# A transformer layer on eight cores: more buffers, one small DMA on another queue, one matmul moved, transposes two deep

## The reference, cut to what matters

```python
q, k, v = (proj(wq), proj(wk), proj(wv))          # 16 heads of 128
q, k = apply_rope(q, k, sin, cos)
att = softmax(einsum('bhqd,bhkd->bhqk', q, k) / sqrt(128))
y = einsum('bhqk,bhkd->bhqd', att, v)
x = _layernorm(x + y @ wo.T)
gate = silu(_qlinear(x, wq_gate, s_gate))         # W = (wq - 128) * scale
up = _qlinear(x, wq_up, s_up)                     # 5632 hidden features
x = _layernorm(x + _qlinear(gate * up, wq_down, s_down))
```

## Time and profile before

| | us |
|---|---|
| device time, the two runs shown | 5102.63 and 5252.95 (median 5177.79) |
| profiled execution, its own time | 5106.49 |
| its span on the slowest core (core 6) | 5104.6; all cores 5094.1 to 5104.6 |
| TensorE busy | 3883.1 (76%) |
| ScalarE, VectorE busy | 1315.2 (26%), 635.9 (12%) |
| mean granted TensorE clock | 0.869 of full |
| V projection and its end | 510 to 912 |
| attention | 912 to 2437 |
| output projection (1024 matmuls, 223.8 us) | 2437 to 2675 |
| first and second half of the feed-forward | 2760 to 3896, 3965 to 5105 |
| TensorE idle before the halves | 99.3 and 220.2 |

### The profile page before, as it was taken

The page is one execution under the profiler, slowest core; times in us unless marked ns, Lnnn a source line. Parts: engine busy times, 40 slices in busy tenths (PEclk is TensorE's granted clock), DMA queues, the critical chain, the costliest instruction groups (busy, mean ns, idle before and its releaser), DMA issues.

```text
span 5104.6 us, 42263 instructions; the slowest of 8 cores (5094.1 to 5104.6 us)
## 1 busy us (share of the span) xinstructions
PE 3883.1 (76%) x15680; PEld 1486.5 (29%) x15680; DVE 635.9 (12%) x1592; ACT 1315.2 (26%) x1073; POOL 393.9 (8%) x744
## 2 busy tenths in 40 slices
PE   4999656677777777777983999998830999998870
PEld 2444222111111111111431444433310444443320
DVE  1222000000000000000220000112121000101122
ACT  0111010333333333333341333310022333320003
POOL 0000000000000000000000000012200000002210
PEclk9999878777777777777996999999965999999985
DMA  6334111100100100100455444434425344434432
GB/s 110 59 81 101 44 41 36 34 13 13 25 13 13 25 13 13 25 13 5 140 179 98 76 80 76 75 63 60 62 71 125 64 79 78 75 67 62 62 50 115
DMA packets 193545, 310.96 MB, mean 61 GB/s; under 512 B 92097, under 2 KB 145474, under 8 KB 184514
## 3 DMA queue, kind: packets, MB, share of 16 engines
q0 software_dynamic: 99392, 188.99, 23.3%
q1 hardware_dynamic: 93954, 119.28, 7.5%
HBM read 412.86 MB, written 58.72 MB: 92 GB/s over the span
## 4 chain that ended last, share of the span: by engine, by line
PE 63%; DMA 20%; issue 6%; ACT 5%; DVE 5%; another core or an unknown queue 1%; DVEq 0%; POOLq 0%; ACTq 0%; SPq 0%; POOL 0%
PE PS L555 12%; PE PS L562 12%; PE PS L453 9%; DMA AB<-wd_c 9%; PE PS L509 6%; PE PS L505 5%; PE PS L468 5%; PE PS L537 4%; PE PS L490 4%; DMA AB<-AB 3%; ACT AB L609 3%; DMA v_sp<-AB 3%; PE PS L493 3%; DMA AB<-x1b 2%; PE PS L576 2%
## 5 line engine op out<-in xcount | busy, mean ns | idle before, releaser
L555 PE MATMUL PS<-AB 128*128 128x512 bf16 x2816 | 625.0, 380 | 319.5 <-DMA AB<-x1b 319.5
L609 ACT ACTIVATE AB<-PS,AB 128x1024 bf16<-128x1024 f32 x512 | 563.5, 1113 | 963.5 <-PE PS L493 963.5
L576 PE MATMUL PS<-AB 128*128 128x512 bf16 x2816 | 654.2, 386 | 99.1 <-DVE AB L763 96.4
L562 PE MATMUL PS<-AB 128*128 128x512 bf16 x2816 | 622.1, 379 | 0.0
L490 PE MATMUL PS<-AB 128*128 128x512 bf16 x512 | 248.5, 485 | 383.8 <-DVE AB L713 360.7
L453 PE MATMUL PS<-AB 128*128 128x512 bf16 x2048 | 444.8, 381 | 65.0 <-DMA AB<-wq_c 65.0
L555 PEld LDWEIGHTS PS<-AB 128*128 128x128 bf16 x2816 | 276.1, 98 | 654.5 <-issue 324.3
L505 PE MATMUL PS<-AB 128*128 128x512 bf16 x896 | 400.6, 447 | 37.2 <-ACT AB L609 37.2
L576 PEld LDWEIGHTS PS<-AB 128*128 128x128 bf16 x2816 | 264.8, 99 | 488.5 <-issue 218.3
L509 PE MATMUL PS<-AB 128*1 128x512 bf16 x896 | 386.1, 431 | 0.0
L562 PEld LDWEIGHTS PS<-AB 128*128 128x128 bf16 x2816 | 275.5, 98 | 332.3
(11 more groups left out here) (69 smaller groups left out, 1767.8 us busy)
## 6 DMA issues: line engine op xcount, KB each, us to landing
AB<-wg_c POOLq DMA_DIRECT2D x88, 512.0 KB, 5.2
AB<-wu_c POOLq DMA_DIRECT2D x88, 512.0 KB, 7.2
AB<-wd_c POOLq DMA_DIRECT2D x352, 128.0 KB, 2.9
AB<-x SPq DMA_DIRECT2D x16, 1024.0 KB, 6.1
x1f<-AB SPq DMA_DIRECT2D x16, 1024.0 KB, 4.0
AB<-x1f SPq DMA_DIRECT2D x16, 1024.0 KB, 4.8
out<-AB SPq DMA_DIRECT2D x16, 1024.0 KB, 3.9
AB<-xT POOLq DMA_DIRECT2D x16, 512.0 KB, 32.6
```

The source lines that it names most:

```text
L555: mm = t.matmul(bank(par * 4 + cch)[:, 0:512], GDQ[par][:, di * 128:(di + 1) * 128], X1T[:, di * 1024 + cch * 512: di * 1024 + (cch + 1) * ...
L562: mm = t.matmul(bank(par * 4 + 2 + cch)[:, 0:512], UDQ[par][:, di * 128:(di + 1) * 128], X1T[:, di * 1024 + cch * 512: di * 1024 + (cch + ...
L576: mm = t.matmul(bank(tt)[:, 0:512], HT[:, h2 * 1024 + tt * 128: h2 * 1024 + (tt + 1) * 128], WDQ[i % 2][:, 0:512], start=(h2 == 0), stop=( ...
L609: sc.activation(PT[u % 4], bank(2 * (u % 2), 2)[:, 0:1024], AF.Exp, bias=CVC[:, 0:1], scale=ASCL).then_inc(s2sc, 1)
```

## The change

It has these parts. Buffer VW is doubled (the second copy lies where the Q and K weights and K tiles were); chunk 1 of wv is loaded when the Q and K projection is over, chunk dc from 2 on when the blocks of chunk dc - 2 have ended. The DMA that spreads the row sums (LQ) goes from POOL's queue to SP's, and SP's K and V loads of head h + 2 are issued behind the LQ copy of head h's last block. The broadcast matmul of block m - 1 stands behind the last matmul of block m instead of at its step u = 4. X1O has three buffers instead of two; to make room, ScalarE's sum in the output projection writes its unused elementwise output to the PSUM half it belongs to, and TensorE waits for the square (s3sq) before it reuses that half. The transposes wait for the one before the previous one (two semaphores), and in the first half they start when 8 of the x1b stores have landed; TensorE and the x1f loads wait for all of them. XR4 has four buffers instead of two, with its offsets moved.

```diff
-OFF_ROUT4 = 16384
-OFF_SUMD4 = 40960
+OFF_ROUT4 = 32768
+OFF_SUMD4 = 57344
-    VW  = bf16(OFF_VW, 128, 8192)
+    VW  = [bf16(OFF_VW, 128, 8192), bf16(OFF_WBUF, 128, 8192)]
-    X1O = [f32(OFF_X1O + i * 8192, 128, 2048) for i in range(2)]
+    X1O = [f32(OFF_X1O + i * 8192, 128, 2048) for i in range(3)]
-    XR4 = [f32(OFF_XRES4 + i * 8192, 128, 2048) for i in range(2)]
+    XR4 = [f32(OFF_XRES4 + i * 8192, 128, 2048) for i in range(4)]
...
         @blk.sync
-            for h in range(NH):
-                if h >= 2:
-                    s.wait_ge(s2pv, 32 * (h - 1))
-                    s.wait_ge(s2kv[h % 2], 32 * (h // 2))
+            for h in (0, 1):
                 s.dma_start(out=KVK[h % 2], in_=kt_sp[h]).then_inc(s2kv[h % 2], 16)
                 s.dma_start(out=KVV[h % 2], ...
+            for m in range(NM):
+                h, c = divmod(m, NCH)
+                s.wait_ge(s2l, m + 1)
+                if m >= 1:
+                    s.wait_ge(s2g1, 16 * m)
+                if m >= 2:
+                    s.wait_ge(s2r, m - 1)
+                s.dma_start(out=LQ[m % 2], in_=LSB[m % 2]).then_inc(s2g1, 16)
+                if c == NCH - 1 and h + 2 < NH:
+                    hh = h + 2
+                    s.wait_ge(s2pv, 32 * (hh - 1))
+                    s.wait_ge(s2kv[hh % 2], 32 * (hh // 2))
+                    s.dma_start(out=KVK[hh % 2], in_=kt_sp[hh]).then_inc(s2kv[hh % 2], 16)
+                    s.dma_start(out=KVV[hh % 2], ...
...
                 if th == 0:
                     s.wait_ge(s3pe, NT)
-                    s.wait_ge(s3spb, 16 * NT)
-                    s.wait_ge(s3spf, 16 * NT)
+                    s.wait_ge(s3spb, 16 * 8)
...
                     gi = th * NDI + dt
-                    if gi >= 1:
-                        s.wait_ge(s4xt, 16 * gi)
+                    if th == 1 and dt == 0:
+                        s.wait_ge(s3spb, 16 * NT)
+                    if gi >= 2:
+                        s.wait_ge(s4xt[gi % 2], 16 * (gi // 2))
                     s.dma_start_transpose(
                         X1T[:, dt * 1024:(dt + 1) * 1024],
                         x1b[th * 1024:(th + 1) * 1024, dt * 128:(dt + 1) * 128],
-                    ).then_inc(s4xt, 16)
+                    ).then_inc(s4xt[gi % 2], 16)
+                if th == 0:
+                    s.wait_ge(s3spf, 16 * NT)
                 for it in range(8 + 2):
                     if it >= 2:
...
                         s.dma_start(out=out_h[g2 * 128:(g2 + 1) * 128, :],
-                                    in_=XR4[g2 % 2]).then_inc(s4out, 16)
+                                    in_=XR4[g2 % 4]).then_inc(s4out, 16)
                     if it < 8:
                         g = th * 8 + it
-                        if it < 2:
+                        if it < 4:
                             s.wait_ge(s4pe, 2 * NHT * (th + 1))
-                        if it >= 2:
-                            s.wait_ge(s4ra, g - 1)
-                            s.wait_ge(s4out, 16 * (g - 1))
+                        if it >= 4:
+                            s.wait_ge(s4ra, g - 3)
+                            s.wait_ge(s4out, 16 * (g - 3))
...
         @blk.gpsimd
             for dc in range(4):
-                if dc >= 1:
-                    g.wait_ge(s1pb, 2 * dc)
-                    g.wait_ge(s1vw, 16 * dc)
-                g.dma_start(out=VW, in_=wv_h[dc]).then_inc(s1vw, 16)
+                if dc == 1:
+                    g.wait_ge(s1pe, 32)
+                    g.wait_ge(s1sp, 16 * 16)
+                if dc >= 2:
+                    g.wait_ge(s1pb, 2 * (dc - 1))
+                    g.wait_ge(s1vw[dc % 2], 16 * (dc // 2))
+                g.dma_start(out=VW[dc % 2], in_=wv_h[dc]).then_inc(s1vw[dc % 2], 16)
...
-                g.wait_ge(s2l, m + 1)
-                if m >= 1:
-                    g.wait_ge(s2g1, 16 * m)
-                if m >= 2:
-                    g.wait_ge(s2r, m - 1)
-                g.dma_start(out=LQ[m % 2], in_=LSB[m % 2]).then_inc(s2g1, 16)
...
         @blk.tensor
-                    if u == 4 and m >= 1:
-                        t.wait_ge(s2g2, 16 * m)
-                        t.matmul(bank(6 + (m - 1) % 2)[:, 0:512], ONRB, RLRB[(m - 1) % 2],
-                                 start=True, stop=True).then_inc(s2bc, 1)
...
                 mm.then_inc(s2pv, 1)
+                if m >= 1:
+                    t.wait_ge(s2g2, 16 * m)
+                    t.matmul(bank(6 + (m - 1) % 2)[:, 0:512], ONRB, RLRB[(m - 1) % 2],
+                             start=True, stop=True).then_inc(s2bc, 1)
...
             for tt in range(NT):
                 if tt >= 2:
                     t.wait_ge(s3ra, tt - 1)
+                    t.wait_ge(s3sq, tt - 1)
...
         @blk.scalar
-                    sc.activation(SD3, ROU[it % 3], AF.Identity, bias=zero_b, scale=1.0,
-                                  accum_out=stat(it % 4, S_SUM))
+                    sc.activation(bank((it % 2) * 4, 4)[:, 0:2048], ROU[it % 3], AF.Identity,
+                                  bias=zero_b, scale=1.0, accum_out=stat(it % 4, S_SUM))
...
-                        if g2 >= 2:
-                            sc.wait_ge(s4out, 16 * (g2 - 1))
-                        sc.activation(XR4[g2 % 2], RO4[g2 % 3], AF.Identity,
+                        sc.activation(XR4[g2 % 4], RO4[g2 % 3], AF.Identity,
```

More of the change, by code:

```diff
@@ L230, in build_program @@
     s1v1 = sem("s1v1"); s1sw = sem("s1sw"); s1v2 = sem("s1v2"); s1sp = sem("s1sp")
-    s1vw = sem("s1vw"); s1pb = sem("s1pb"); s1scb = sem("s1scb"); s1spb = sem("s1spb")
+    s1vw = [sem("s1vwA"), sem("s1vwB")]; s1pb = sem("s1pb"); s1scb = sem("s1scb"); s1spb = sem("s1spb")
     s2kv = [sem("s2kvA"), sem("s2kvB")]; s2st = sem("s2st"); s2pv = sem("s2pv"); s2sc = sem("s2sc")
@@ L238, in build_program @@
     s3spf = sem("s3spf"); s3spb = sem("s3spb")
-    s4xt = sem("s4xt"); s4w = [sem("s4wA"), sem("s4wB")]; s4dq = sem("s4dq"); s4pe = sem("s4pe")
+    s4xt = [sem("s4xtA"), sem("s4xtB")]; s4w = [sem("s4wA"), sem("s4wB")]; s4dq = sem("s4dq"); s4pe = sem("s4pe")
     s4sil = sem("s4sil"); s4stt = sem("s4stt"); s4wd = [sem("s4wdA"), sem("s4wdB")]; s4wq = sem("s4wq")
@@ L301, in _ @@
                             in_=v_sp[:, :, h * 128:(h + 1) * 128].rearrange("k p b -> p k b")).then_inc(s2kv[h % 2], 16)
+            for m in range(NM):
[11 more added lines that the diff above has]
+                    s.dma_start(out=KVK[hh % 2], in_=kt_sp[hh]).then_inc(s2kv[hh % 2], 16)
+                    s.dma_start(out=KVV[hh % 2],
+                                in_=v_sp[:, :, hh * 128:(hh + 1) * 128].rearrange("k p b -> p k b")).then_inc(s2kv[hh % 2], 16)
             if DEBUG:
@@ L324, in _ @@
                         s.wait_ge(s3spf, 16 * sp)
-                    s.dma_start(out=x1f[sp * 128:(sp + 1) * 128, :], in_=X1O[sp % 2]).then_inc(s3spf, 16)
+                    s.dma_start(out=x1f[sp * 128:(sp + 1) * 128, :], in_=X1O[sp % 3]).then_inc(s3spf, 16)
             if PH < 4:
@@ L355, in _ @@
                         s.dma_start(out=out_h[g2 * 128:(g2 + 1) * 128, :],
-                                    in_=XR4[g2 % 2]).then_inc(s4out, 16)
+                                    in_=XR4[g2 % 4]).then_inc(s4out, 16)
                     if it < 8:
                         g = th * 8 + it
-                        if it < 2:
+                        if it < 4:
                             s.wait_ge(s4pe, 2 * NHT * (th + 1))
-                        if it >= 2:
-                            s.wait_ge(s4ra, g - 1)
-                            s.wait_ge(s4out, 16 * (g - 1))
+                        if it >= 4:
+                            s.wait_ge(s4ra, g - 3)
+                            s.wait_ge(s4out, 16 * (g - 3))
                         if g >= 1:
                             s.wait_ge(s4x, 16 * g)
-                        s.dma_start(out=XR4[g % 2], in_=x1f[g * 128:(g + 1) * 128, :]).then_inc(s4x, 16)
+                        s.dma_start(out=XR4[g % 4], in_=x1f[g * 128:(g + 1) * 128, :]).then_inc(s4x, 16)
             s.wait_ge(s4out, 16 * NT)
@@ L418, in _ @@
                     g.wait_ge(s3spb, 16 * tt)
-                g.dma_start(out=x1b[tt * 128:(tt + 1) * 128, :], in_=X1O[tt % 2]).then_inc(s3spb, 16)
+                g.dma_start(out=x1b[tt * 128:(tt + 1) * 128, :], in_=X1O[tt % 3]).then_inc(s3spb, 16)
             if PH < 4:
@@ L461, in _ @@
                 if th == 0:
-                    t.wait_ge(s1vw, 16 * (dc + 1))
+                    t.wait_ge(s1vw[dc % 2], 16 * (dc // 2 + 1))
                 if jb >= 1:
@@ L469, in _ @@
                                       XT[:, di * 2048 + tg * 128: di * 2048 + (tg + 1) * 128],
-                                      VW[:, di * 512:(di + 1) * 512],
+                                      VW[dc % 2][:, di * 512:(di + 1) * 512],
                                       start=(di == 0), stop=(di == NDI - 1))
@@ L545, in _ @@
             for th in range(2):
```

(16 more changed lines are left out.)

## The result

The changed kernel takes 5032.1 us (median of 11 runs, 4925.7 to 5387.9) beside 5236.7 us (median of 10, 5102.6 to 5289.7) for the kernel before on the same chip. The prediction was 4920 us with a range of 4850 to 4995. On a second chip (run e4_after_again) it was 4935.8 us beside 5109.6, a ratio of 0.966, interval 0.964 to 0.967. So the kernel is faster on both chips; that it is so by more than 2% is clear on the second one only.

What follows compares the result with a forecast made beforehand. It took hand-offs between engines and queues, not the matmul streams inside big stages, to bound the kernel. Its terms, 14 + 94 + 27 + 27 + 24 = 186 us, off 5106.5 us gave 4920, range 4850 to 4995.

Steps and rivals of the forecast that it cites:

- V projection: TensorE's gaps at changes of weights: only the third loses its colliding wv load, two stay long; gain 14 us.
- The row-sum copy on SP: Attention's block ends: reciprocal waits 2.05 us instead of 2.80 with LQ issued from SP; 0.75 us per block, 47 us.
- Heads' ends: Attention, where a head ends: LQ ahead of K and V cuts the reciprocal's 4.75 us wait; 14 x 1.95 = 27 us.
- the late semaphore: Attention's heads' ends: if the row-sum copy's completion stays late despite the new order, that gain is 0.
- The broadcast: Attention: the one-row matmul, moved from mid-block into TensorE's idle time, saves 0.32 us in 63 blocks, 20 us.
- Output projection: TensorE's added wait for the square of two tiles before is covered with 3.6 us to spare; cost nothing.
- Transposes: Ahead of both feed-forward halves: two in flight, 1.67 us each, first half also starting 8 us earlier; 27 us each half.
- Tails: Normalisation tails: the x1f load no longer waits for the store's landing; less 2 us contention, 2 us in 12 waits, 24 us.
- One: Attention: the issuing queue does not matter, LQ lands as late from SP; 4967 us, chance 0.13.
- two: Transposes: two in flight land no sooner than one by one, only the 8 us start remains; 4966 us, chance 0.12.
- four: Attention: LQ from SP lands as late as the v_sp gather, 5.5 us; slower, 5156 us, chance 0.02.
- Three, the clock: Attention: shorter idle keeps TensorE at 2.4 GHz in a fifth of the blocks, up to 64 us; 4856 us, chance 0.14.

Runs made afterwards that it cites:

- experiment 9: Changed kernel with the broadcast back at step u = 4 and VectorE multiplying block m - 1 in the middle of block m; 4566.6 us (median of 4).
- experiment 6: Changed kernel with wv chunks 2 and 3 loaded only after the v_sp stores of the chunk before them have landed; 4900.0 us.
- experiment 4: Kernel before, with only SP's K and V loads held until the LQ copy, still on POOL's queue, has landed; 5106.6 us.
- experiment 5: Changed kernel with each transpose again waiting for the one before, the early start in the first half kept; 4973.2 us.
- experiment 7: Changed kernel with SP issuing the first four x1f loads of each tail ahead of the first out store; 4850.0 us, best of 3.
- experiments 2: Kernel before, with only the LQ copy on SP's queue and the K and V loads behind it; 5173 to 5266 us, attention 1450 to 1457.
- experiment 3: Kernel before, with only the broadcast matmul moved behind the block's last matmul; attention 1485 to 1490 us, 1486 on core 6 against 1525.
- experiment 8: Changed kernel with POOL holding gate and up weights from the second hidden tile on until 14 of 16 transposes have landed; 4908.5 us.

## Why the prediction was right or wrong

**The numbers.** This is the step that failed. It set 4920 and an upper end of 4995 from waits and transfers alone, on a profiled execution in which no core was granted the 0.8125. The two times shown were 5102.6 and 5253.0; the text noted that the profile agreed with the lower and that the median was their mean, and left it there. The 150 us between them had no term and no rival. They came back in the changed kernel: 514 us instead of 444 for a stage that the change does not touch, and a median of 5032 us. Executions without it were 4925.7, 4937.3 and 4941.4 us, and 4935.8 is the median on the second chip. An upper end that took in half of the spread of the two times, 75 us, would have stood at 5070. The chance of 0.93 for faster by over 2% stood on the same step; on the first chip the interval reaches to 0.984.

**What bounds the kernel** was read rightly: every wait named from the earlier trace rows moved. That the matmul streams inside the big stages are hardly touched was wrong for attention: its matmuls were busy 28 us less with the change, and 150 us less again in experiment 9.

**V projection.** 14 us predicted, 21 measured on core 6, and 14.5 as the mean of the eight cores (368.4 before, 353.9 after). The mechanism is shown, two gaps at 26 and one at 13 us, and experiment 6 shows that the load makes the store late.

**The row-sum copy on SP.** 0.75 us a block predicted, 0.51 measured. The estimate of 0.12 us for the hand-off was near (0.18); the size of the landing, 1.93 us, was wrong: it is 2.11, no faster than from POOL. Taking 0.5 us off the rope copy for its data was the step at fault. Nearest came the estimate of 0.4 us a block that the prediction set beside its sum, but the trace has the difference ahead of the issue and not in the landing. The copy's wait fell by 62 us where 74 were predicted for both parts on it.

**Heads' ends.** 4.75 to 2.29 us: the mechanism holds, and the late semaphore does not. Of its 31 us of waits only 9 reached attention's length when done alone, since some 25 us came back as matmuls at 1.2 GHz (experiment 4).

**The broadcast.** 20 us predicted; 22 us in waits and 13 us in faster matmuls, 39 in attention. Together the three parts were predicted at 94 and gave 111: the waits alone 80, the clock 26. The sum came near because a term that was too large and a term that was missing offset each other.

**Output projection.** 0 predicted, 0 measured (223 us both times); TensorE has no wait for the square.

**Transposes.** Second half 27 predicted; the 16 shrank by 53.3 - 32.0 = 21 us: in the end 2.0 us each, where 1.67 was forecast. First half 27 predicted, 17 measured. The step at fault is the 8 us for the early start, worth nothing by experiment 5; the two-deep issue took 22.6 us off the transposes there, so all of the gain is its.

**Tails.** 2 us in each of 12 steps predicted, 1.4 measured (120.7 against 138.0 us of wait): the load is issued 3.98 - 0.49 = 3.49 us sooner behind the store, but it takes 6.7 us instead of 4.8 beside it (median of the page's DMA issues) and the add comes 2.0 us later. The 2 us of contention were right; the issue's own 0.49 us was left out. That the order of issue, not the buffers, bounds the tails was right, and experiment 7 shows its price: 110 us.

**The rivals.** One and two fell (experiments 2, 5), four as well (the reciprocal's wait became shorter, not longer). Three, the clock, came in part: attention's mean clock went from 0.79 to 0.81, and the matmuls gave 26 us of the 64 it had for a fifth of the blocks. Experiment 9 shows what stood behind it: with the idle time at blocks' ends gone altogether, 150 us more.

## What to carry to other kernels

Give the run-to-run spread that the measured times show a term of its own before summing waits; it outweighed every error of size here. Price an engine's hand-off and its transfer apart, from the releaser's end to the issue and from the issue to the reader. And ask of a chain that ends a wait not how to shorten each link but who has to stand behind it: moving one multiply ahead of the wait gave 380 us in attention, twice what the whole change gave.

## What the chip showed that was not expected

- The cost of a matmul in attention moved between 0.342 and 0.359 us (its busy time over 3136) when only waits of some us between blocks were changed, and fell to 0.295 us when none was left at blocks' ends. In the five kernels that have the gap, attention's time on core 6 at 2.4 GHz stayed at 874 to 877 us while its length went from 1525 to 1414. A wait shortened by 2 us at heads' ends gave some 25 us of matmul time back (experiment 4).
- In two executions (the changed kernel's and experiment 3's) two cores of a die ran the whole Q/K projection at clock 0.83 and the two others at 1.00; these had the same 0.8125 only from 4539 and 4688 us of their spans on. The other die never had it.
- POOL takes 0.70 us from a releaser's end to its issue, SP 0.18; from the issue of the same 2 KB to its reader it is 2.10 and 2.11 us.
- The last store ahead of the second half's transposes is issued 12 to 13 us before they start, before the change (3898.1 to 3910.1) and after (3741.5 to 3754.1), where a store in mid-tail lands in 4 us. With the weight loads held back it takes 4.1 us (experiment 8).
